# Moving small VectorE arithmetic to GpSimd, ScalarE and identity matmuls in a fused patch-embed, causal-attention and top-16-attention kernel

## What is computed

```python
# 1. tokens: 32 x 32 patches of 16 x 16 over the image and four shifted copies, then layer-norm, then a dense layer
y = conv(concat([x, right, left, down, up]), conv_w, stride=16) + conv_b        # (8, 1024, 128)
h = concat([layernorm(y, 1e-3) * gamma + beta) @ dense_w + dense_b, txt])       # (8, 1101, 128)
# 2. causal attention, 8 heads of 64, on xn = layernorm(h)
h = h + (softmax(causal(q @ k.T / 8)) @ v) @ W_out + b_out + xn
# 3. top-16 attention, 8 heads of 16, on xn = layernorm(h)
x = xn + depthwise_conv3(xn, pos_w) + pos_b
logits = (q * 128 ** -0.5) @ k.T                         # (64, 1101, 1101)
_, idx = top_k(logits, 16)                               # each row keeps its 16 largest
h = h + (softmax over those 16, times v[idx]) @ wo_w.T + wo_b
```

## Time and profile before

| | |
|---|---|
| median of 3 runs | 4133.57 us (4127.76 to 4135.05) |
| the profiled execution | 4142.41 us; span from first to last instruction 4140.6 us |
| busy share of the span | VectorE 86%, TensorE 83%, ScalarE 55%, GpSimd 44% |
| instructions | 92,874 |

### The profile page before, as it was taken

How to read it: one execution, slowest core, us unless ns; L and a number is a source line. 1 busy time by engine, 2 the same in 40 slices (tenths; PEclk the granted TensorE clock), 3 DMA queues, 4 the chain that set the end, 5 groups by cost and what they waited for, 6 DMA issues and landing times.

```text
span 4140.6 us, 92874 instructions
## 1 busy us (share of the span) xinstructions
PE 3434.1 (83%) x34936; PEld 2239.0 (54%) x34936; DVE 3575.8 (86%) x5062; ACT 2268.4 (55%) x5793; POOL 1829.9 (44%) x2985
## 2 busy tenths in 40 slices
PE   4877788988988899988998899988988788975555
PEld 4645555555556555555555565555555455543333
DVE  0222599999999999999999999999999999999997
ACT  1655455655665566656665566655665556642222
POOL 2333444454444544454444544454444544442222
PEclk7999999999999999999999999999999999987777
DMA  5200300021100300021100310021000200010000
GB/s 78 52 5 3 88 20 3 3 53 33 25 3 9 79 20 13 8 52 30 20 13 8 79 23 10 4 53 33 15 5 2 60 15 2 2 41 18 13 1 6
DMA packets 233210, 103.54 MB, mean 25 GB/s; under 512 B 195441, under 2 KB 210242, under 8 KB 232770
## 3 DMA queue, kind: packets, MB, share of 16 engines
q1 hardware_dynamic: 228448, 95.64, 10.3%
q10 hardware_dynamic: 4322, 1.97, 0.4%
HBM read 78.86 MB, written 18.67 MB: 24 GB/s over the span
## 4 chain that ended last, share of the span: by engine, by line
DVE 46%; issue 24%; PE 16%; POOL 8%; SPq 3%; ACT 2%; ACTq 0%; DMA 0%; DVEq 0%; POOLq 0%
DVE A L1546 13%; DVE top L1551 10%; DVE M L1560 9%; DVE top L1539 8%; PE bank_ps L988 3%; DVE newmax L1492 3%; POOL PB L912 2%; PE bank_ps L1104 2%; POOL M L946 2%; PE score_ps L1076 2%; PE bank_ps L1167 2%; PE bank_ps L1173 2%; PE logit_ps L1145 1%; ACT PB L1302 1%; DVE negmax L1489 1%
## 5 line engine op out<-in xcount | busy, mean ns | idle before, releaser
L946 POOL TENSOR_SCALAR M<-M,to_mark 128x1101 bf16<-128x1101 bf16 x576 | 731.3, 1270 | 1209.8 <-DVE M L1560 1199.8
L1383 ACT ACTIVATE PT<-bank_ps 128x512 f32<-128x512 f32 x1296 | 755.7, 600 | 676.9 <-PE bank_ps L1173 673.0
L1539 DVE MAX8 top<-logit_ps 128x8 f32<-128x1101 f32 x576 | 749.4, 1301 | 93.9 <-PE logit_ps L1145 93.5
L1551 DVE MAX8 top<-A 128x8 f32<-128x1101 f32 x576 | 749.5, 1301 | 7.3 <-issue 0.2
L1546 DVE MATCH_REPLACE8 A<-top,logit_ps 128x1101 f32<-128x1101 f32 x576 | 746.6, 1296 | 0.9 <-issue 0.9
L1560 DVE MATCH_REPLACE8 M<-top,A 128x1101 bf16<-128x1101 f32 x576 | 744.1, 1292 | 1.2 <-issue 1.2
L1167 PE MATMUL bank_ps<-stack 128*128 128x512 bf16 (+5 forms) x1728 | 571.6, 345 | 131.4 <-POOL M L946 111.6
L1302 ACT ACTIVATE PB<-score_ps,negmax 128x512 f32<-128x512 f32 (+3 forms) x896 | 527.1, 595 | 197.9 <-DVE negmax L1489 131.7
L1321 ACT COPY PTc<-bank_ps 128x512 f32<-128x512 f32 (+2 forms) x800 | 424.7, 546 | 273.8 <-PE bank_ps L988 271.0
L1173 PE MATMUL bank_ps<-turn_m,M 128*128 128x128 bf16 (+1 forms) x5184 | 571.2, 226 | 0.0
L1076 PE MATMUL score_ps<-qk 64*128 64x512 f32 (+4 forms) x1920 | 446.1, 541 | 113.7 <-ACT PB L1302 111.3
(11 more groups left out here) (144 smaller groups left out, 4062.5 us busy)
## 6 DMA issues: line engine op xcount, KB each, us to landing
stack<-qk_parts SPq DMA_DIRECT2D x512, 72.0 KB, 2.7
X<-in_x SPq DMA_DIRECT2D x248, 60.8 KB
X<-in_x SPq DMA_DIRECT2D x248, 57.0 KB
qk_parts<-OT SPq DMA_DIRECT2D x16, 864.0 KB, 5.1
Wp<-in_L_attn_W_in SPq DMA_DIRECT2D x96, 64.0 KB, 2.0
out<-H SPq DMA_DIRECT2D x8, 512.0 KB
X<-in_x SPq DMA_DIRECT2D x248, 3.6 KB
stack<-in_L_tok_conv_w ACTq DMA_DIRECT2D x30, 64.0 KB
```

Source lines behind the costliest of these rows:

```text
L946: nc.gpsimd.tensor_scalar(M[:, n % M_SLOTS, :], M[:, n % M_SLOTS, :], to_mark[:, 0:1], to_mark[:, 1:2], ALU.mult, ALU.add).then_inc(marked, 1)
L1383: nc.scalar.activation(PT[0:rows, q % P_SLOTS, :], where[0:rows, :], ACT.Exp).then_inc(free(group), 1)
L1539: nc.vector.max(top[:, n % M_SLOTS, 0:8], logit_ps[:, 0:L]).then_inc(top8, 1)
L1551: nc.vector.max(top[:, n % M_SLOTS, 8:16], A[:, n % 2, :]).then_inc(top16, 1)
```

## The change

Six pieces of arithmetic leave VectorE.

- Layer-norm statistics: the aggregating instruction (L1461) is gone. `var` is made on GpSimd from the raw statistics with 6 small instructions, 5 of them followed by a wait, `newton` on GpSimd with 5; the shift is no longer computed (normalising subtracts the mean, then multiplies).
- Running minimum (L1497) is gone: each piece is exponentiated against its own maximum. GpSimd's `gap` takes the least of a row's 2 or 3 maxima with two small instructions and a wait before it forms the gaps, now one for every piece; `correct`, `total` and `scale` treat the last piece like the others.
- Residual (`add_res`): TensorE adds H with an identity matmul behind each tile's output projection, and ScalarE copies the bank out. The first `res` of an image now waits for `resid_done`.
- Final residual (`add_out`): the same with H1, and the first `outp` waits for `wo_added`.
- Positional convolution: `pos0` has two more ScalarE instructions, which write the two scaled neighbours into the q and v buffers of causal attention (qk[:, 1] and qk[:, 2]); `pos1` and `pos2` become plain additions on GpSimd. The next image's copy of v waits for `pos_done`.
- The planner's costs and dependencies follow, so the order of every engine is made anew.

```diff
-            add("DVE", 0.45, due + 4, ("stat_t", c, i), ("copy_y", c, i))
+            add("DVE", 0.28, due + 4, ("stat_t", c, i), ("copy_y", c, i),
+                *([("var_t", c - 1)] if c else []))
-        add("DVE", 0.2, due, ("var_t", c), *[("stat_t", c, i) for i in range(NPT)])
+        add("POOL", 1.2, due, ("var_t", c), *[("stat_t", c, i) for i in range(NPT)])
-        add("DVE", 1.0, due, ("newton_t", c), ("ln_t", c), *([("normal_t", c - 1, NPT - 1)] if c else []))
+        add("POOL", 1.2, due, ("newton_t", c), ("ln_t", c), *([("normal_t", c - 1, NPT - 1)] if c else []))
...
-                add("DVE", 2 * w * 0.00105 + 0.15 + (0.2 if j else 0), due + 1, ("rowmax", *f), ("scores", *f),
+                add("DVE", 2 * w * 0.00105 + 0.15, due + 1, ("rowmax", *f), ("scores", *f),
-                        add("POOL", 0.2, due + 3, ("gap", c, p, i), ("rowmax", *f))
+                        add("POOL", 0.7, due + 3, ("gap", c, p, i), ("rowmax", *f))
...
-        add("ACT", 1.1, due + 13, ("pos0", c), *[("copy_2", c, g) for g in range(3)],
+        add("ACT", 3.9, due + 13, ("pos0", c), *[("copy_2", c, g) for g in range(3)],
-        add("DVE", 1.4, due + 14, ("pos1", c), ("pos0", c))
-        add("DVE", 1.4, due + 14, ("pos2", c), ("pos1", c))
+        add("POOL", 2.4, due + 14, ("pos1", c), ("pos0", c))
+        add("POOL", 2.4, due + 14, ("pos2", c), ("pos1", c))
...
+                elif event in ("var_t", "var_1", "var_2"):
+                    pool.wait_ge(measured[k], n * (c + 1))
...
+                    settle_ln(nc.gpsimd.tensor_tensor(v, m_even, m_odd, ALU.subtract))
+                    settle_ln(nc.gpsimd.tensor_tensor(v, v, v, ALU.mult))
+                    settle_ln(nc.gpsimd.tensor_scalar(v, v, D / 4, D * (TOK_EPS if k == 0 else EPS), ALU.mult, ALU.add))
+                    settle_ln(nc.gpsimd.tensor_tensor(v, v, s_even, ALU.add))
+                    settle_ln(nc.gpsimd.tensor_tensor(mean[:, k, 0:n], m_even, m_odd, ALU.add))
+                    nc.gpsimd.tensor_tensor(v, v, s_odd, ALU.add).then_inc(var_known[k], 1)
+                elif event in ("newton_t", "newton_1", "newton_2"):
...
+                    settle_ln(nc.gpsimd.tensor_scalar(mean[:, k, 0:n], mean[:, k, 0:n], 0.5, 0.0, ALU.mult, ALU.add))
+                    pool.wait_ge(guessed[k], nth("ln_" + event[-1], c))
+                    settle_ln(nc.gpsimd.tensor_tensor(w, v, y, ALU.mult))
+                    settle_ln(nc.gpsimd.tensor_tensor(w, w, y, ALU.mult))
+                    settle_ln(nc.gpsimd.tensor_scalar(w, w, -0.5 / D, 1.5, ALU.mult, ALU.add))
+                    nc.gpsimd.tensor_tensor(rstd[:, k, 0:n], y, w, ALU.mult).then_inc(rstd_known[k], 1)
...
+                    for hh in range(2):
+                        of_pieces = [negmax[:, s, j, hh:hh + 1] for j in range(J + 1)]
...
+                            last = nc.gpsimd.tensor_scalar(least[:, s, hh:hh + 1], of_pieces[0], of_pieces[1], of_pieces[2],
+                                                           ALU.min, ALU.min)
+                    last.then_inc(least_known, 1)
+                    pool.wait_ge(least_known, nth("gap", c, p, i))
...
+                            by = fix[:, s, j, hh:hh + 1] if J else 1.0
...
+                elif event == "pos1":
+                    pool.wait_ge(pos_first, c + 1)
+                    nc.gpsimd.tensor_tensor(xpT[:, 1:L], xpT[:, 1:L], qk[:, 2, 0:L - 1], ALU.add).then_inc(pos_v, 1)
...
+                    if t == 0:
+                        pe.wait_ge(resid_done, c + 1)
...
+                    last = nc.tensor.matmul(where[:, q0:q0 + 128], ident[:, :], H[:, t, :], start=False, stop=True)
...
+                    if g == 0:
+                        pe.wait_ge(wo_added, c + 1)
...
+                        last = nc.tensor.matmul(at, ident[:, :], H1[:, c % 2, t, :], start=False, stop=True)
...
+                    nc.scalar.mul(qk[:, 2, 0:L - 1], x2T[:, 0:L - 1], cols[:, 2:3])
+                    nc.scalar.mul(qk[:, 1, 0:L - 1], x2T[:, 1:L], cols[:, 4:5]).then_inc(pos_first, 1)
...
-                    settle(nc.vector.bn_stats(st[:, k, i, :], src))
-                    nc.vector.bn_aggr(mv[:, k, i, :], st[:, k, i, :]).then_inc(ln_v, 1)
-                    small["ln"] += 1
...
+                    nc.vector.bn_stats(st[:, k, i, :], src).then_inc(measured[k], 1)
...
-                        nc.vector.tensor_tensor(negmax[:, s, j, :], newmax[:, :], negmax[:, s, j - 1, :], ALU.min
-                                                ).then_inc(rowmax, 1)
+                    nc.vector.reduce_max(negmax[:, s, j, :], score_v[:, :, 0:z - a], AX.X, negate=True
+                                         ).then_inc(rowmax, 1)
```

More of the change, by code:

```diff
@@ L279, in make_plan @@
         for i in range(NT):
-            add("DVE", 0.45, due + 5, ("stat_1", c, i), ("bias_h", c, i // 4) if i < NPT else ("load_txt", c))
-        add("DVE", 0.2, due + 5, ("var_1", c), *[("stat_1", c, i) for i in range(NT)])
+            add("DVE", 0.28, due + 5, ("stat_1", c, i), ("bias_h", c, i // 4) if i < NPT else ("load_txt", c),
+                *([("var_1", c - 1)] if c else []))
+        add("POOL", 1.2, due + 5, ("var_1", c), *[("stat_1", c, i) for i in range(NT)])
         add("ACT", 0.45, due + 5, ("ln_1", c), ("var_1", c))
-        add("DVE", 1.0, due + 5, ("newton_1", c), ("ln_1", c), *([("normal_1", c - 1, NT - 1)] if c else []))
+        add("POOL", 1.2, due + 5, ("newton_1", c), ("ln_1", c), *([("normal_1", c - 1, NT - 1)] if c else []))
         for i in range(NT):
@@ L563, in build @@
         st = sb("st", [128, 3, NT, 6])
-        mv = sb("mv", [128, 3, NT, 2])
+        mean = sb("mean", [128, 3, NT])
         vareps = sb("vareps", [128, 3, NT])
@@ L568, in build @@
         rstd = sb("rstd", [128, 3, NT])
-        shift = sb("shift", [128, 3, NT])
         negmax = sb("negmax", [128, 2, 3, 2])
-        newmax = sb("newmax", [128, 2])
-        gaps = sb("gaps", [128, 2, 2, 2])
-        fix = sb("fix", [128, 2, 2, 2])
+        least = sb("least", [128, 2, 2])
+        gaps = sb("gaps", [128, 2, 3, 2])
+        fix = sb("fix", [128, 2, 3, 2])
         rowsum = sb("rowsum", [128, 2, 3, 2])
-        sums = sb("sums", [128, 2, 2, 2])
+        sums = sb("sums", [128, 2, 3, 2])
         rinv = sb("rinv", [128, 2, 2])
@@ L638, in build @@
         logit_done = sem("logit_done")
+        measured = [sem(f"measured{k}") for k in LN]
         var_known = [sem(f"var_known{k}") for k in LN]
@@ L1114, in _ @@
                     q0 = 128 * (t % 4)
+                    if t == 0:
+                        pe.wait_ge(resid_done, c + 1)
                     for q in range(NP):
-                        last = nc.tensor.matmul(where[:, q0:q0 + 128], OT[:, q, 128 * t:128 * t + 128], Wo1[:, q, :],
-                                                start=(q == 0), stop=(q == NP - 1))
+                        nc.tensor.matmul(where[:, q0:q0 + 128], OT[:, q, 128 * t:128 * t + 128], Wo1[:, q, :],
+                                         start=(q == 0), stop=False)
+                    last = nc.tensor.matmul(where[:, q0:q0 + 128], ident[:, :], H[:, t, :], start=False, stop=True)
                     if t in (3, 7, 8):
@@ L1208, in _ @@
                     copied(pe, *[("turn_o", c, gg) for gg in range(g, min(g + 2, 3))])
+                    if g == 0:
+                        pe.wait_ge(wo_added, c + 1)
                     for q, t in enumerate(WG[g]):
-                        last = nc.tensor.matmul(where[:, 128 * q:128 * q + 128], OcT[:, 128 * t:128 * t + 128],
-                                                WT[:, 3, :], start=True, stop=True)
+                        at = where[:, 128 * q:128 * q + 128]
+                        nc.tensor.matmul(at, OcT[:, 128 * t:128 * t + 128], WT[:, 3, :], start=True, stop=False)
+                        last = nc.tensor.matmul(at, ident[:, :], H1[:, c % 2, t, :], start=False, stop=True)
                     last.then_inc(done(e), 1)
@@ L1281, in _ @@
                         act.wait_ge(split_done, nth("split3", c - 1, s))
+                    if c > 0 and (p, s, g) == (0, 2, 0):
+                        act.wait_ge(pos_done, c)
                     if s < 2:
@@ L1327, in _ @@
                     nc.scalar.copy(OT[:, p, 128 * i:128 * i + 128], where[:, 0:128]).then_inc(free(group), 1)
+                elif event == "add_res":
+                    g, = of
+                    group = ("res", c, g)
+                    where = filled(act, group)
+                    if c >= 2:
+                        act.wait_ge(stored[c % 2], 32 * (c // 2))
+                    t0, t1 = WG[g][0], WG[g][-1] + 1
+                    nc.scalar.copy(H1[:, c % 2, t0:t1, :].rearrange("p t d -> p (t d)"), where[:, 0:128 * (t1 - t0)]
+                                   ).then_inc(free(group), 1)
+                elif event == "add_out":
+                    g, = of
+                    group = ("outp", c, g)
+                    where = filled(act, group)
```

(11 more changed lines are left out.)

120 lines of the change are left out of this document (45 added, 75 removed).

## The result

The changed kernel takes 4190.74 us (median of 4 runs, 4189.7 to 4195.01), the kernel before 4132.14 in the same session: 1.0142 times as long, 95% interval 1.0127 to 1.0157. The forecast was 4078, in a range from 4000 to 4138.

What follows compares the result with a forecast made beforehand. The prediction took VectorE to bound A, and VectorE's nearly full list together with the chain to the next image's logits to bound B. From 4133.6 us, -61 + 0 + 5 = -56 gave 4078, range 4000 to 4138.

Steps and rivals of the forecast that it cites:

- What leaves VectorE: Work taken off VectorE: 19.3 us an image, 9.7 from A and 9.6 from B; 154 us over eight images.
- A: -8.7 us: Seven stretches of 397.6 us, VectorE 95.0% busy: each loses 8.7 us of a possible 9.7, together -61 us.
- B: "no change": Seven stretches of 69.3 us, from causal attention's last piece to the next image's first logits: saved VectorE time becomes idle.
- the working's 7.1 of slack: In B, the logits start 7.1 us after quarter 0 of the stack lands.
- The chain of B: +4.8 us: Longer chain in B: var +1.5, newton +0.3, pos0 +2.6, positional additions +0.2, identity matmul +0.2 us.
- Start and end: +5 us: First 454 us: minima -4.9, layer-norms +5.4, positional step +2.8; last output projection +2.1; together about +5, between -5 and +10.
- Rival 3, "GpSimd's list decides B", 4176,: GpSimd's added work stands ahead of the logits, B grows by 14 us, total 4176 us; chance 0.10.
- agrees on the price: For GpSimd's positional additions, the trace was said to agree with the skill's two-times price: 2.63 against 1.78 us.
- Rival 1: VectorE's whole saving counts in A and B: 135 us go, +5 at start and end, 4004 us; chance 0.24.
- rival 2: TensorE takes over in A, which keeps its length: 4139 us, between 4115 and 4165; chance 0.13.
- The sum: Whole kernel: -61 for A, 0 for B, +5 for start and end, -56 us, giving 4078 us.

Runs made afterwards that it cites:

- add_mult_chain: The changed kernel with the mean kept negated, normalising by (add, multiply), and the planner's chain due at 50 steps, not 58: 4078.74 us, ratio 0.9869.
- experiment 2: The changed kernel with normalising back at (multiply by rstd, add shift), the shift made on GpSimd by one more small instruction: 4149.32 us, ratio 1.0033.
- experiment 1: The kernel before with one edit, GpSimd normalising by (subtract mean, multiply by rstd) in place of (multiply, add): 4183.31 us, ratio 1.0113.
- experiment 5: The changed kernel with the planner's chain behind causal attention due at 50 of 72 steps, not 58, same instructions: 4142.40 us, ratio 1.0015.
- experiment 9: The changed kernel with normalising by (multiply, add), the chain due at 50 steps, and the positional step as before the change: 4096.15 us, ratio 0.9909.
- experiment 10: The changed kernel with normalising by (multiply, add), chain due at 50 steps, and the planner's stack lag 3 us, not 12: 4115.20 us, ratio 0.9955.
- experiment 11: The changed kernel normalising by four forms of the instruction by tile number, multiply paired with add or subtract in either order: 4179.0 us in one run.

## Why the prediction was wrong

- **What leaves VectorE.** Right, a little large: 135.8 us of the forecast 154.
- **A: -8.7 us.** The mechanism was right and the size too large in the changed kernel, -6.5. With the two losses mended it is -10.0 (add_mult_chain), which is the forecast's upper bound of 9.7 and a little.
- **B: "no change".** This is the step that failed: +11.1 us, seven times. It had two holes. First, the working priced what moves to GpSimd, but not the instruction there whose operations the diff changed. Normalising stands in the earlier trace rows with 3.92 us for 9 tiles; with a subtraction it takes 7.03, and that costs B 4.6 us (experiment 2) to 5.3 (experiment 1). Second, it took the order of the lists as it was. The planner's costs were changed in the same diff, and in the new order the last `res` came 5 us later after `place` and the first logits stood behind two score pieces of the next image, where images 2 to 4 had none; another order of the same instructions gives B 4.1 us (experiment 5). In image 2 the stack landed 12.4 us later, where 4.8 were forecast, and the 6.8 us from there to the logits (the working's 7.1 of slack) grew to 9.0. Without both losses, B is 70.5 to 71.3, within 2 us of "no change".
- **The chain of B: +4.8 us.** To the end of `split3` it grew by 51.8 - 41.1 = 10.7: normalising starts 5.2 later (the order, by experiment 5 all but 0.4, though 2.0 were forecast for `var`, `newton` and the identity matmul) and takes 3.1 longer; the positional step takes 5.1 longer, where 2.8 were forecast; the splits win 2.7 back. The additions were priced right at 2.52 each. What was missed is that a mark ran ahead of `pos1` and the bias of the next image (1.28 us) between `pos1` and `pos2`, and that the stack's issue waits in the DMA queue's list too: it came 13.6 later.
- **Start and end: +5 us.** Measured: +14.9 in the start, of which 12.1 are the form of the normalising (469.1 - 457.0); without it +2.8, against the working's -4.9 + 5.4 + 2.8 = +3.3.
- **Rival 3, "GpSimd's list decides B", 4176,** came nearest, with a chance of 0.10. B was over 77 us (80.5), ahead of the turn of the maxima TensorE waited for GpSimd's normalising, and GpSimd's work in a B rose by 14.7 us (45.4 to 60.1), where 11.3 were forecast. But its prices were for the additions and the small steps, and these were not the loss: with them on GpSimd, the normalising by addition and multiplication, and the chain due earlier, the change is faster by 1.3%. And behind GpSimd stood TensorE's list, 13.4 us from the turn to the logits in image 2. The Trainium skill's rule on elementwise work (GPSIMD Engine Reference, section 4.1 Engine selection) does not explain the loss either: it speaks of the price, about two times on two inputs. The traces show the direction and less of it, 2.52 us for a plain addition against 1.78 for VectorE's multiplication and addition, so the prediction's "agrees on the price" was generous; and putting the two additions back on VectorE gained nothing, in an order made anew (experiment 9).
- **Rival 1 and rival 2.** Neither came about. TensorE's busy time in A is unchanged (2486.7 of 2486.6 us).
- **The sum.** -61 + 0 + 5 became -45 + 78 + 15 in the profiled execution. With the two losses mended (add_mult_chain) the same sum reads -70 + 8 + 2 = -60, and the time is 4078.74 us. That this is the forecast's number is luck: it is the time of another kernel, in which A gained more than forecast and B lost what was put at nothing.

What stays open: which of the moved events gives each part of the 4 us of B in experiment 5, since no run moves one alone; why the two repairs together give A 1 us an image more than their sum; and how far TensorE's clock (below) adds to the wait.

## What to carry to other kernels

Price every instruction that the diff touches, also those that stay on their engine: one with the same shape and count, and another operation, was worth 41 to 47 us here, and a sign moved into an operand takes it away. Where a planner makes the order, a change of its costs is a change of the kernel: look where each step of the chain stands in the new lists, the DMA queue's too, and give the critical chain an earlier due time before judging the arithmetic. And judge an order by whole periods, since experiment 10 moved 6 us out of B and 10 into A.

## What was not expected of the hardware

- On GpSimd the instruction with two operations on 128x128 f32 takes 447 to 453 ns with multiplication and addition in either order, and 802 to 803 ns when one of the two is a subtraction (medians, experiment 11).
- The least of two maxima, 128x1 with the second as a pointer, takes 277 ns there, more than a subtraction of 128x2 by two tensors (196); with three it takes 364:

```profile
L929 POOL TENSOR_SCALAR least<-negmax 128x1 f32<-128x1 f32 x256 | 68.0, 277 | 180.4 <-DVE negmax L1540 180.4
...
L931 POOL TENSOR_SCALAR least<-negmax 128x1 f32<-128x1 f32 x64 | 22.5, 364 | 30.8 <-DVE negmax L1540 30.8
```

- TensorE's clock fell while TensorE waited for normalising. In the B shown, TensorE was busy for 0.44 us of 4 and then for 1.35 of 4 while GpSimd made layer-norm 2, and from 1824 the granted clock was 0.50, the lower of its two levels; it was back at 1.00 from 1832 (windows: length, busy time of PE, granted clock). In the same step of add_mult_chain, from 1768 to 1790, it stayed at 1.00.

```profile
1816.00:1820.00 4.00, 0.44 (x3) 1.00 0.03 10
1820.00:1824.00 4.00, 1.35 (x7) 0.67 0.01 2
1824.00:1828.00 4.00, 1.09 (x4) 0.50 0.00 0
1828.00:1832.00 4.00, 3.43 (x17) 0.55 0.00 0
1832.00:1836.00 4.00, 3.70 (x34) 1.00 0.00 0
```
